# Graph network, attention stage by pairs of visits: one maximum, correction and sum for two visits of a node block

## The reference, cut to what matters

```python
h = jnp.maximum(_layernorm(x), 0.0)
x = x + _L1_gnn_ref(h, edge_index, edge_attr_16, ...)

lin_x = x @ W_lin.T + b_lin
feat = jnp.concatenate([x[src], edge_weights, x[dst]], axis=1)
h = jax.nn.relu(feat @ W_att1.T + b_att1)                # 144 wide
scores = (h @ W_att2.T + b_att2)[:, 0]
m = jax.ops.segment_max(scores, src, num_segments=num_nodes)
e = jnp.exp(scores - m[src])
denom = jax.ops.segment_sum(e, src, num_segments=num_nodes)
alpha = e / denom[src]
msg = jax.ops.segment_sum(alpha[:, None] * lin_x[dst], src, num_segments=num_nodes)
```

## Time and profile before

| | |
|---|---|
| median of three runs | 7030.38 us (7029.48 to 7033.46) |
| profiled execution, its own time | 7037.61 us, its span 7035.8 us |
| busy over the whole span | PE 4939.3 us (70%), DVE 4627.5 us (66%), ACT 1961.5 us (28%), POOL 4964.8 us (71%) |
| stage C, the loop | 4852 to 6918 us of the span |

### The profile page before, as it was taken

How to read it: one execution, slowest core, us unless ns; L and a number is a source line. 1 busy time by engine, 2 the same in 40 slices (tenths; PEclk the granted TensorE clock), 3 DMA queues, 4 the chain that set the end, 5 groups by cost and what they waited for, 6 DMA issues and landing times.

```text
span 7035.8 us, 172631 instructions
## 1 busy us (share of the span) xinstructions
PE 4939.3 (70%) x30025; PEld 3731.2 (53%) x30026; DVE 4627.5 (66%) x20348; ACT 1961.5 (28%) x5229; POOL 4964.8 (71%) x10449
## 2 busy tenths in 40 slices
PE   6444667676644666666766666666888888888887
PEld 2333444444643544455544444444777777777775
DVE  5777888888643643333333333335999999999997
ACT  4000000000000332222222222223555555555555
POOL 1677777777777367777777777776777777777775
PEclk9555555555555777767678877787888888888888
DMA  8333333333432134333333333334333333333333
GB/s 270 63 56 58 54 59 55 59 55 59 74 63 53 54 119 122 111 110 109 105 105 105 106 106 105 106 105 127 93 93 93 93 93 93 93 93 94 92 93 93
DMA packets 1146494, 649.15 MB, mean 92 GB/s; under 512 B 798449, under 2 KB 1050339, under 8 KB 1145572
## 3 DMA queue, kind: packets, MB, share of 16 engines
q1 hardware_dynamic: 1006804, 412.21, 24.0%
q0 software_dynamic: 137728, 233.30, 11.7%
q10 hardware_dynamic: 1888, 2.83, 0.2%
HBM read 360.75 MB, written 311.42 MB: 96 GB/s over the span
## 4 chain that ended last, share of the span: by engine, by line
issue 20%; POOL 17%; PE 12%; DVE 5%; DMA 4%; ACT 3%; POOLq 2%; DVEq 1%; ACTq 0%; SPq 0%
PE banks L1359 7%; POOL rows_by_src L829 6%; DMA rows_by_src<-ring 3%; PE banks L1405 1%; POOL ring L874 1%; POOL ring L890 1%; ACT ring L1054 1%; POOL ring L871 1%; ACT ring L1047 1%; POOL ring L869 1%; PE banks L1360 1%; POOL ring L882 1%; POOL ring L863 1%; DVE wide L1974 1%; PE banks L1347 1%
## 5 line engine op out<-in xcount | busy, mean ns | idle before, releaser
L829 POOL DMA_INDIRECT rows_by_src<-ring x1760 | 1712.9, 973 | 553.1 <-issue 491.6
L801 POOL DMA_INDIRECT wide<-msg_table,ring x1664 | 1580.3, 950 | 681.7 <-issue 491.3
L1359 PE MATMUL banks<-wide,ring 128*128 x3520 | 1290.0, 495 | 472.4 <-ACT ring L1047 375.8
L1273 PE MATMUL banks<-wide,ring 128*128 x3520 | 860.1, 426 | 512.3 <-DMA wide<-msg_table,ring 256.3
L1359 PEld LDWEIGHTS banks<-wide,ring 128*128 128x128 f32 x3520 | 748.9, 263 | 743.5 <-issue 694.1
L1273 PEld LDWEIGHTS banks<-wide,ring 128*128 128x128 f32 x3520 | 784.2, 328 | 591.6 <-issue 591.0
L1941 DVE COPY ring<-ring 128x4 f32<-128x4 f32 x440 | 82.0, 186 | 1138.4 <-DMA rows_by_src<-ring 1138.2
L1054 ACT COPY ring<-banks 128x416 f32<-128x416 f32 x880 | 402.5, 510 | 1440.7 <-PE banks L1360 1440.7
L1405 PE MATMUL banks<-wide,ring 128*128 x5328 | 718.4, 266 | 0.0
L1726 DVE TENSOR_TENSOR acc<-acc,banks 128x64 f32 x1760 | 389.7, 221 | 499.2 <-PE banks L1273 284.2
L1405 PEld LDWEIGHTS banks<-wide,ring 128*128 128x128 bf16 x5328 | 549.4, 110 | 112.4 <-issue 0.2
(11 more groups left out here) (326 smaller groups left out, 9820.6 us busy)
## 6 DMA issues: line engine op xcount, KB each, us to landing
wide<-rows_by_src SPq DMA_DIRECT2D x1776, 105.0 KB, 2.0
ring<-attr_turned SPq DMA_DIRECT2D x440, 128.0 KB
attr_turned<-ring SPq DMA_DIRECT2D x416, 96.0 KB
rows_by_src<-ring POOLq DMA_INDIRECT x1760
wide<-msg_table,ring POOLq DMA_INDIRECT x1664
ring<-attr_by_dst SPq DMA_DIRECT2D x208, 64.0 KB
attr_turned<-ring SPq DMA_DIRECT2D x208, 64.0 KB
attr_by_dst<-in_edge_attr_dram SPq DMA_DIRECT2D x1, 13281.2 KB
```

What stands on the lines that cost most here:

```text
L801: g.indirect_dma_start(out=A_g[:, b * GV + u, :], out_offset=None, in_=table[:, :], in_offset=bass.IndirectOffsetOnAxis(ap=A_idx[:, b * GV ...
L829: g.indirect_dma_start(out=rows_d[:, :], out_offset=bass.IndirectOffsetOnAxis(ap=B_pos[:, s, u:u + 1], axis=0), in_=B_row[:, s, u, :], in_ ...
L1273: last = mm(bank[s][:, u * HID:(u + 1) * HID], A_D[:, s, u, :], A_g[:, ds(r[u], 1), :].rearrange("p a k -> p (a k)"), start=True, stop=True)
L1359: mm(b, B_DT[:, t, u, :], qh[:, w, :].rearrange("p a k -> p (a k)"), start=True, stop=False)
```

## The change

Visits come in pairs of the same window. In the table each window's number of visits is rounded up to an even number (the extra visit meets no edge of its window in its tile), so the bound on the visits grows: `C_VISITS` goes from 1776 to 1872, 78 iterations instead of 74, 468 ticks instead of 444. A tick is still four visits, now two pairs (`PV` = 2):

- DVE's maximum (L2005) goes over 256 columns at a time, gives two values and not four, and writes them to PSUM (bank 5); the scan (L2015) runs over two values and reads these from PSUM.
- POOL's operations on penalties, maxima and corrections work on two values instead of four. None of its instructions goes.
- PE's sums by node (L1420) of a pair go to one place in PSUM, the second added to the first. The correction of PE's maxima is sent per visit as before.
- DVE has two `add_sums` per tick instead of four.
- The window numbers for stage C are kept per pair; PE and DVE load two registers per tick instead of four.
- `visit_table(1)` has three more small operations, and works over 1872 columns; the first table now has 1760 columns instead of 1776.

```diff
-C_VISITS = C_BODY * -(-VISITS // C_BODY)
+C_VISITS = C_BODY * -(-(-(-N_EDGES // P) + N_WIN - 1 + N_WIN) // C_BODY)
...
+PV = GV // 2
...
+        C_tm = bank[5][:, 4 * GV:4 * GV + PV]
...
# POOL
-                    m_pen = ch.do(g.tensor_tensor(C_pen[:, s, :], wbase_all[:, ds(n, GV)], wbase[:, ds(n, GV)], ALU.subtract))
+                    m_pen = ch.do(g.tensor_tensor(C_pen[:, s, :], of_pairs(wbase_all[:, ds(n, GV)]), of_pairs(wbase[:, ds(n, GV)]), ALU.subtract))
...
-                    m_hi = ch.do(g.tensor_tensor(mp[0], new, C_zero, ALU.add))
+                    m_hi = ch.do(g.tensor_tensor(mp[0], new, C_zero[:, 0:PV], ALU.add))
...
# PE
-                    r = regs(ENG.PE, wwin, j1 * C_BODY + t1 * GV, N_WIN - 1)
+                    r = regs(ENG.PE, wpair_of, j1 * (C_BODY // 2) + t1 * PV, N_WIN - 1, PV)
...
-                        w = p_tab[:, ds(r[u], 1), :].rearrange("p a k -> p (a k)")
+                        w = p_tab[:, ds(r[u // 2], 1), :].rearrange("p a k -> p (a k)")
...
-                        last = mm(bank[6 + t % 2][:, u * (HID + 1):(u + 1) * (HID + 1)], C_S[:, t, u, :], C_W[:, t % 2, u, :],
-                                  start=True, stop=True)
+                        last = mm(bank[6 + t % 2][:, (u // 2) * (HID + 1):(u // 2 + 1) * (HID + 1)], C_S[:, t, u, :], C_W[:, t % 2, u, :],
+                                  start=u % 2 == 0, stop=u % 2 == 1)
...
# DVE, visit_table(1)
+                    ch.link(v.tensor_scalar(ei, t1, 1.0, None, ALU.add))
+                    ch.link(v.tensor_scalar(ei, ei, 1, None, ALU.arith_shift_right))
+                    ch.link(v.tensor_copy(t1, ei))
+                    v.scalar_tensor_tensor(nt[0:K, :], t1, 2.0, hs, ALU.mult, ALU.mult).then_inc(s_vcols, 1)
...
# DVE, tick
-                if 6 in stages:
-                    ch.need(m_acc)
-                    m_acc = ch.do(add_sums(1))
                 if 3 in stages:
                     t3, j3 = stages[3]
                     after_c(dve, c_MKt, t3, j3)
-                    m_tm = ch.do(v.tensor_reduce(C_tm[:, t3, :], four(bank[4], P), AX.X, ALU.max))
+                    m_tm = ch.do(v.tensor_reduce(C_tm, two(bank[4], 2 * P), AX.X, ALU.max))
                 if 6 in stages:
                     ch.need(m_acc)
-                    m_acc = ch.do(add_sums(2))
+                    add_sums(1).then_inc(c_acc, 1)
...
-                    v.tensor_tensor_scan(C_mn[:, 1 + k:1 + k + GV], C_pen[:, t3, :], C_tm[:, t3, :], C_mn[:, k:k + 1],
+                    v.tensor_tensor_scan(C_mn[:, 1 + k:1 + k + PV], C_pen[:, t3, :], C_tm, C_mn[:, k:k + 1],
                                          ALU.add, ALU.max).then_inc(c_new, 1)
-                if 6 in stages:
-                    ch.need(m_acc)
-                    add_sums(3).then_inc(c_acc, 1)
```

More of the change, by code:

```diff
@@ L285, in build @@
         d_place = planes[3]
-        low_b, high_b, tile_rel = (acc_flat[:, 900 * k:900 * k + 888].bitcast(bf16) for k in range(3))
-        tile_is = [acc_flat[:, 900 * k:900 * k + 888].bitcast(bf16) for k in (3, 4)]
+        low_b, high_b, tile_rel = (acc_flat[:, 900 * k:900 * k + VTAB // 2].bitcast(bf16) for k in range(3))
+        tile_is = [acc_flat[:, 900 * k:900 * k + VTAB // 2].bitcast(bf16) for k in (3, 4)]
         b_parts = acc_flat[0:1, 4600:4600 + PARTS * BIAS // 2].bitcast(bf16).rearrange("a (k n) -> a k n", k=PARTS)
@@ L337, in build @@
         C_kl = part(ring, CS * GV // 2, RING).bitcast(bf16).rearrange("p (s u) -> p s u", s=CS)
-        C_mp = part(ring, CS * GV * PARTS // 2, RING).bitcast(bf16).rearrange("p (s u k) -> p s u k", s=CS, u=GV)
-        C_raw, C_s, C_r, C_tm, C_pen, C_mo, C_mr, C_df, C_cr, C_mg, C_z, C_d, C_p = (marks(CS) for _ in range(13))
+        C_mp = part(ring, CS * PV * PARTS // 2, RING).bitcast(bf16).rearrange("p (s u k) -> p s u k", s=CS, u=PV)
+        C_raw, C_s, C_r, C_mg, C_z, C_d, C_p = (marks(CS) for _ in range(7))
+        C_pen, C_mo, C_mr, C_df, C_cr = (part(ring, CS * PV, RING).rearrange("p (s u) -> p s u", s=CS) for _ in range(5))
         C_zero, C_step = part(ring, GV, RING), part(ring, GV, RING)
-        C_mn = part(ring, 1 + CS * GV, RING)
+        C_mn = part(ring, 1 + CS * PV, RING)
         at[0] = 0
@@ L1208, in visit_tables @@
                 for q in range(4):
-                    m = vmask[0:HW, q * VCHUNK:(q + 1) * VCHUNK]
-                    mm(bank[q][:, 0:VCHUNK], ones[0:HW, :], m, start=True, stop=True)
-                    last = mm(bank[4 + q][:, 0:VCHUNK], dbc[0:HW, :], m, start=True, stop=True)
+                    m = vmask_of[k][0:HW, q * n:(q + 1) * n]
+                    mm(bank[q][:, 0:n], ones[0:HW, :], m, start=True, stop=True)
+                    last = mm(bank[4 + q][:, 0:n], dbc[0:HW, :], m, start=True, stop=True)
                 last.then_inc(s_vsums, 1)
@@ L1379, in tick @@
                     for u in range(GV):
-                        last = mm(bank[5][:, u * PARTS:(u + 1) * PARTS], C_STb[:, t, u, :], C_mp[:, t, u, :], start=True, stop=True)
+                        last = mm(bank[5][:, u * PARTS:(u + 1) * PARTS], C_STb[:, t, u, :], C_mp[:, t, u // 2, :], start=True, stop=True)
                     last.then_inc(c_mm, 1)
```

53 lines of the change are left out of this document (31 added, 22 removed).

## The result

| | before | after |
|---|---|---|
| median of four runs | 7031.92 us (7029.48 to 7036.77) | 7230.87 us (7230.23 to 7234.23) |
| profiled execution, its span | 7035.8 us | 7228.0 us |
| granted clock, mean of the span | 0.714 | 0.689 |

The ratio is 1.0283, with an interval of [1.0265, 1.0301]: slower by 199 us. The forecast was 7115 us, +84 us, in a range of 7055 to 7160. The direction was right, the size was missed by 116 us.

A forecast was written before the change was run, and what follows sets the result against it. A loop closed within one tick, through POOL, DVE's one-hots and L1998 and ACT's exponent, was taken as the bound. Ticks +110.8, savings -27.3 and table +1 made +84.5 us on the 7030.4 median: 7115 us, range 7055 to 7160.

The forecast's parts named there:

- More ticks: Stage C: 24 more ticks, four iterations of 27.7 us, real work on every engine; +110.8 us.
- Register loads of two values: Between DVE's one-hots and first add_sums, mostly covered by the one-hots; 0 to 0.05 us per tick, taken as zero.
- the loop that the prediction itself had named as the one that closes: Within one tick: POOL's fifteen instructions, DVE's one-hots, one add_sums and L1998, ACT's exponent; sets the tick, 4.615 us.
- Two `add_sums` fewer: DVE in stage C: 0.41 us per tick less work, of which 0.25 us per iteration was taken as gain.
- POOL's two values: POOL's small operations on two values, not four: 0.03 us per tick at most; 0.10 us per iteration taken.
- the wait before L857: POOL's wait for ACT's L1071, 0.50 us per tick; said to cover time the one-hots would hold L857 up anyway.
- Maximum and scan in PSUM: DVE's maximum written to and scan read from PSUM: between -0.41 and +0.1 us, beside POOL's 2.75 us; zero.
- PE's products about 1.2 us: PE's 12 products, six register computations fewer: 1.6 us becomes about 1.2 at the higher clock; no gain by itself.
- The table: Ahead of stage C: three more operations of 0.16 us and 1872 columns for 1776; +1 us.
- A: Rival: DVE's instructions set the tick, 0.41 us go from each; -81 us, 6950 us; chance 0.06.
- B: Rival: the loop over two ticks through PE, DVE, ACT and POOL bounds; +15 us, 7045 us; chance 0.12.
- C: Rival: PE's low-clock stretches come twice as often, 30% more ticks cost up to 0.25 us; +120, 7150 us; chance 0.10.

The follow-up runs named there:

- pair_four: Changed kernel with a per-visit window table, aligned register loads of four values, every second used, and 80 unused columns; 7169.84 us, ratio 1.0190.
- before_two_adds: Kernel before without add_sums(1) and add_sums(3), half of the sums left out of its result; 7029.22 us, ratio 0.9994.
- pair_four_scores: pair_four with the scores' weights also read from a copy in PSUM; 7096.4 us, ratio 1.0076 to the kernel before.

## Why the prediction was wrong

*More ticks, +110.8.* Right: 24 of them, and before's tick was 4.615 us.

*Register loads of two values, "from 0 to 0.05 us per tick. Zero".* **This step failed.** It priced the load by its count, fewer registers and so no more time, and took the one-hots as its cover. The load went from 0.34 to 0.53 us, none of the difference was covered (DVE idle ahead of L1988 in 458 ticks), and the `add_sums` and L2016 came later by 0.19 us, on the loop that the prediction itself had named as the one that closes. pair_four against the changed kernel puts it at 62.6 us, over half of the 108 us by which the spans missed the forecast. The upper bound of 0.05 had no row under it. The trace of before gives the load of four outright in the view of its line, 0.34 us, and no row shows one of two values; a form that no row shows should have been bounded from both sides, say by half and by twice that. And the cover, which I took for large, was already overdrawn: 0.12 + 0.34 + 0.27 = 0.73 us, where the next instruction could start at 0.61. The earlier trace rows hinted at it with 80.1 us of idle time ahead of L1970, most of it without a named cause, and the timeline behind the earlier trace rows with an addition 0.84 us behind the start of the one-hots.

*Two `add_sums` fewer and POOL's two values, -27.3.* The mechanism held and its size did not. DVE was not the bound (before_two_adds, 0.9994; pair_four_scores, 0.012 us a tick), and its idle time moved in front of the one-hots. But the small gain that I let through did not come: pair_four, without the load's cost, runs at 4.629 us a tick and not 4.557, 34 us over the stage. Earlier scores meet POOL's six small operations (0.97 to 1.09 us in pair_four). And once L866 no longer waits for the scores, it and L869 run beside the one-hots: together they take 679 ns in pair_four and 715 in the changed kernel, where L857 and L860 took 508. I had written of the wait before L857 that it "covers time in which L857 would be held up by the one-hots anyway", and did not ask what else on POOL earlier DVE work would hold up. POOL's operations on two values gave nothing: they take 0.19 to 0.20 us where nothing holds them up, as those on four do.

*Maximum and scan in PSUM, zero; PE's products about 1.2 us, zero.* Right: L2020 takes 691 ns (L2005 684), the scan 212 in place of 291. The twelve products take 1.04 us in place of 1.60 at the higher clock (forecast 1.2) and 1.65 in both kernels at the lower, as medians; the eight products of L1420 take the same whether they add up or not, 1.11 us at the higher clock and 1.97 at the lower.

*The table, +1.* Right as far as it goes; stage B's 12.6 us were in no step, and I can't say what should have shown them.

*The rivals.* A (DVE the bound) and B (the two-tick loop) are out: before_two_adds should have gained 182 us by A and 91 by B and gained nothing, DVE's idle time grew, and the wait of B's loop, in front of L866, fell to a third while the tick grew. C's condition came true in part: the granted clock fell from 0.85 to 0.76, so the share of time at the lower level went from 30% to 48%. Its price did not: in the changed kernel's trace the 47 ticks that lie at the lower clock as a whole take 4.66 us on average, and the 154 at the higher one 4.87; before, 4.41 and 4.65. And pair_four_scores, at 0.78, runs at 4.469 us a tick, less than before's 4.615 at 0.85. No run sets the clock by itself, so this rules out C's sum and not every effect of the clock.

The sum, from the forecast to the spans: 84.5, and 62.6 for the load, 34 for gains that did not come, 12 for stage B, is 193, against 192 measured. It splits the loss in the order in which pair_four took it; with the scores in PSUM first, the load's part would be 29.

## What to carry to other kernels

A change that takes work from an engine which is not the bound still moves everything that this engine does in time; ask of each instruction that moves what it will run beside, and whether the two can run together. Price what looks like bookkeeping: a register load is an instruction of 0.3 to 1 us, and its form (how many values, from which position) is part of the change. Where DVE and POOL work beside each other on SBUF, a constant operand of DVE's copied once to PSUM took 53 us off the kernel before and 106 off the changed one (by medians).

## What the runs showed of the hardware

- A register load from SBUF on DVE took 0.34 us for four values that start on a multiple of four, 0.53 for two wherever they start, and up to 0.99 for four that start in the middle; on PE 0.33, 0.54 and 1.01. Which partition the table is in made no difference (0.529). The Trainium skill, "Runtime: NRT & Kernel Launch", section "Instruction fetch mechanics", gives about 200 ns per register for such loads from HBM; no run here loads from HBM. From SBUF two registers took longer than four, so a price per register does not fit, and the measurement decides.
- The instruction that needs the registers came 0.27 us behind the end of the load, and the load started 0.12 us behind the start of the instruction ahead of it; 0.69 us of one-hots did not cover a load of 0.34.
- DVE instructions of the same duration (0.30 us) stretched POOL's 128x2 operations from starts 0.15 us apart to 0.23 when both their inputs were in SBUF, and not at all when one was in PSUM.
- Each of 1760 scatters took 6 ns longer in the kernels with pairs, at lines that the change leaves as they were; unexplained.
